# Compressed interaction network on one core: two of the three layers' sums over d move from VectorE to ScalarE

## The reference

```python
x0 = embeddings                       # (B=2048, M=32, D=16), gathered from 32 tables
xk = x0
for W in (W0, W1, W2):                # (32, 32, 64), (32, 64, 64), (32, 64, 64)
    xk = relu(einsum('bmd,bhd,mhk->bkd', x0, xk, W))
    outs.append(sum(xk, axis=2))      # sum over d
z = concatenate(outs, axis=1)         # (2048, 192)
h = relu(concatenate([z, dense_ctx], axis=1) @ W_top1 + b_top1)   # 512
h = relu(h @ W_top2 + b_top2)                                     # 256
y = h @ W_top3
```

## Time and profile before

| | |
|---|---|
| median of 3 runs | 1193.18 us (1192.31 to 1193.81) |
| profiled execution | 1192.97 us, its span 1191.2 us |
| granted TensorE clock, mean over the span | 0.991 |
| busy, share of the span | PE 94%, DVE 94%, ACT 62%, POOL 77% |

### The profile page before, as it was taken

The page is one execution under the profiler, slowest core; times in us unless marked ns, Lnnn a source line. Parts: engine busy times, 40 slices in busy tenths (PEclk is TensorE's granted clock), DMA queues, the critical chain, the costliest instruction groups (busy, mean ns, idle before and its releaser), DMA issues.

```text
span 1191.2 us, 14658 instructions
## 1 busy us (share of the span) xinstructions
PE 1121.3 (94%) x5312; PEld 393.6 (33%) x5312; DVE 1118.8 (94%) x521; ACT 733.9 (62%) x1361; POOL 918.8 (77%) x640
## 2 busy tenths in 40 slices
PE   0488899999999999999999999999999999999997
PEld 0122223333333333333333333333333333333333
DVE  0487999999999999999999999999999999999995
ACT  0343666676667667665766766576676657657653
POOL 6688888888888888888888888888888888885400
PEclk9888999999999999999999999999999999999999
DMA  5887787667678766677876666788666778876300
GB/s 110 190 176 146 158 171 155 138 132 144 140 157 171 157 141 141 132 144 150 172 163 136 143 134 145 144 171 168 139 140 134 143 145 169 166 144 144 61 1 1
DMA packets 76216, 167.25 MB, mean 140 GB/s; under 512 B 21776, under 2 KB 39072, under 8 KB 76144
## 3 DMA queue, kind: packets, MB, share of 16 engines
q1 hardware_dynamic: 59216, 161.95, 64.8%
q0 software_dynamic: 16384, 4.23, 3.6%
q10 hardware_dynamic: 544, 0.14, 0.1%
HBM read 157.86 MB, written 8.40 MB: 140 GB/s over the span
## 4 chain that ended last, share of the span: by engine, by line
PE 86%; POOL 3%; DVE 3%; DMA 3%; issue 3%; ACT 1%; SPq 1%; DVEq 0%
PE acc L600 80%; POOL x_rows L254 3%; DVE p_dve L516 3%; PE acc L672 3%; PE acc L658 1%; PE acc L660 1%; DMA q_tile<-x_of_steps 1%; ACT xb L317 1%; DMA x_rows<-in_table,ids_s 1%; PE acc L680 1%; DMA spread<-x_of_steps 1%; SPq L192 1%; DMA x_of_steps<-x_rows 0%; SPq L219 0%; DVE z L543 0%
## 5 line engine op out<-in xcount | busy, mean ns | idle before, releaser
L600 PE MATMUL acc<-p_dve,w_s 128*64 128x512 f32 x3840 | 863.2, 598 | 22.5 <-DVE p_dve L516 21.8
L254 POOL DMA_INDIRECT x_rows<-in_table,ids_s x512 | 493.7, 964 | 146.1 <-issue 131.2
L516 DVE TENSOR_TENSOR p_dve<-spread,xb 128x3072 f32<-128x3072 f32 (+2 forms) x224 | 572.2, 2682 | 2.9 <-issue 2.9
L516 DVE TENSOR_TENSOR p_dve<-spread,xa 128x2048 f32<-128x2048 f32 (+1 forms) x192 | 501.5, 2730 | 16.6 <-issue 9.1
L600 PEld LDWEIGHTS acc<-p_dve,w_s 128*64 128x64 f32 x3840 | 267.9, 137 | 571.5 <-issue 467.2
L317 ACT ACTIVATE xb<-acc 32x512 f32<-32x512 f32 x512 | 288.8, 564 | 71.6 <-DVE p_dve L516 65.5
L266 POOL TENSOR_TENSOR p_l<-spread,q_tile 128x2048 f32<-128x2048 f32 x60 | 272.7, 4573 | 11.0 <-DMA q_tile<-x_of_steps 10.4
L308 ACT ACTIVATE xa<-acc 64x512 f32<-64x512 f32 x256 | 145.9, 570 | 189.6 <-PE acc L600 155.0
L277 POOL TENSOR_TENSOR p_pool<-spread,x_s 128x1024 f32<-128x1024 f32 x64 | 152.2, 2378 | 94.7 <-PE acc L600 45.9
L600 PE MATMUL acc<-p_l,w_s 128*64 128x512 f32 (+1 forms) x640 | 152.5, 612 | 41.6 <-DVE p_l L556 41.6
L326 ACT ACTIVATE x_s<-acc 64x512 f32<-64x512 f32 x256 | 151.5, 592 | 8.3 <-ACT y_row L449 4.8
(11 more groups left out here) (18 smaller groups left out, 151.1 us busy)
## 6 DMA issues: line engine op xcount, KB each, us to landing
spread<-x_of_steps SPq DMA_DIRECT2D x248, 512.0 KB, 17.4
q_tile<-x_of_steps SPq DMA_DIRECT2D x128, 128.0 KB, 11.4
x_rows<-in_table,ids_s POOLq DMA_INDIRECT x512
x_of_steps<-x_rows SPq DMA_DIRECT2D x64, 128.0 KB
spread<-x_of_steps SPq DMA_DIRECT2D x16, 256.0 KB, 5.4
w_s<-in_w SPq DMA_DIRECT2D x2, 512.0 KB, 5.7
wt<-in_w_top SPq DMA_DIRECT2D x1, 512.0 KB, 6.5
z_all<-in_dense_t ACTq DMA_DIRECT2D x16, 8.0 KB, 8.2
```

What stands on the lines that cost most here:

```text
L254: nc.gpsimd.indirect_dma_start(out=x_rows[:, s % 2, i * DIM:(i + 1) * DIM], out_offset=None, in_=table, in_offset=bass.IndirectOffsetOnAxi ...
L516: nc.vector.tensor_tensor(p_dve[:, to:to + n, :], spread[:, s % 3, tile:tile + n, :], over(x[:], n), ALU.mult).then_inc(dve_made, n)
L600: last = nc.tensor.matmul(acc[b * K:(b + 1) * K, :], w, prod[:, b * BLK:(b + 1) * BLK], start=start, stop=stop)
```

## The change

Layers 0 and 1 (the first and the second) get their sums on ScalarE. Instead of one eviction of 512 columns, 32 evictions of 16 columns each are issued, every one with an accumulator output that gives the sum of its 16 results to one column of `z`. In the built program each such eviction is two ScalarE instructions, the ACTIVATE and one that writes the accumulator's value to `z`; the listing of the order below has one row for both. VectorE keeps only the sums of the third layer (`sums_2`). `sums(s, 0)` stands behind `x1_b(s)` where `out_0(s)` stood ahead of it, `x2_a(s-1)` stands ahead of `out_2(s-2)`, the accumulators are given back by `z_made` in place of `out_ready`, and the MLP's first two stages move from behind chunk 5 to behind chunk 8 of L1.

```diff
-MLP1_AFTER, MLP2_AFTER, MLP3_AFTER = 5, 5, 13
+MLP1_AFTER, MLP2_AFTER, MLP3_AFTER = 8, 8, 13
...
-            def out_0(s):
+            def sums(s, layer, acc):
                 if s > 0:
-                    act.wait_ge(z_made[0], s)
-                nc.scalar.activation(out_l[:, 0, :], acc0[:], ACT.Relu).then_inc(out_ready[0], 1)
+                    act.wait_ge(z_made[layer], s)
+                if s % 2 == 0 and s >= 4:
+                    act.wait_ge(z_moved, s // 2 - 1)
+                for i in range(SB // 2):
+                    cols = slice(i * DIM, (i + 1) * DIM)
+                    last = nc.scalar.activation(out_l[:, layer, cols], acc[:, cols], ACT.Relu,
+                                                accum_out=z[:, s // 2 % 2, layer, s % 2, i:i + 1])
+                last.then_inc(z_made[layer], 1)
...
                 x1_b(s)
+                sums(s, 0, acc0)
+                if s >= 1:
+                    x2_a(s - 1)
                 if s >= 2:
                     out_2(s - 2)
-                if s >= 1:
-                    x2_a(s - 1)
...
                     x2_s(s - 1)
-                    out_1(s - 1)
+                    sums(s - 1, 1, acc1[(s - 1) % 2])
...
                     x1_a(s + 1)
                     x1_s(s + 1)
-                    out_0(s + 1)
...
                 for c, n in GROUPS_L1:
-                    if c == NT:
-                        sums(s, 0)
-                        if s >= 2:
-                            sums(s - 2, 1)
...
                     if c == 0 and s > 0:
                         pe.wait_ge(x1b_ready, s)
-                        pe.wait_ge(out_ready[0], s)
+                        pe.wait_ge(z_made[0], s)
```

More of the change, by code:

```diff
@@ L153, in build_kernel @@
         x2b_ready = sem("x2b_ready")
-        out_ready = [sem(f"out{n}_ready") for n in range(3)]
+        out2_ready = sem("out2_ready")
         z_made = [sem(f"z{n}_made") for n in range(3)]
@@ L388, in x2_s @@
                 relu_s(acc1[s % 2], 2, x2s_ready)
[L390 to L394, removed]
             def out_2(s):
@@ L400, in out_2 @@
                     act.wait_ge(z_made[2], s)
-                nc.scalar.activation(out_l[:, 2, :], acc2[:], ACT.Relu).then_inc(out_ready[2], 1)
+                nc.scalar.activation(out_l[:, 2, :], acc2[:], ACT.Relu).then_inc(out2_ready, 1)
             def move_sums(t, to, k, n):
@@ L457, in _ @@
             x1_s(0)
-            out_0(0)
             for s in range(STEPS):
@@ L492, in _ @@
             x2_s(STEPS - 1)
-            out_1(STEPS - 1)
+            sums(STEPS - 1, 1, acc1[(STEPS - 1) % 2])
             mlp3(TILES - 2)
@@ L536, in layer2, with sums_2 @@
                 products(s, 2, c, n)
-            def sums(s, n):
+            def sums_2(s):
                 if s % 2 == 0 and s >= 4:
                     dve.wait_ge(z_moved, s // 2 - 1)
[L542 to L545, removed]
+                dve.wait_ge(out2_ready, s + 1)
+                nc.vector.reduce_sum(z[:, s // 2 % 2, 2, s % 2, :],
+                                     out_l[:, 2, :].rearrange("p (i d) -> p i d", d=DIM),
+                                     AX_X).then_inc(z_made[2], 1)
             def first_layer_products(s):
@@ L581, in _ @@
                 if s >= 2:
-                    sums(s - 2, 2)
+                    sums_2(s - 2)
                 if s >= 1:
@@ L587, in _ @@
                 if c == NT:
[L588 to L591, removed]
+                    sums_2(STEPS - 2)
                 layer2(STEPS - 1, c, n)
-            sums(STEPS - 1, 2)
+            sums_2(STEPS - 1)
         @block.tensor
@@ L622, in layer1 @@
                 if c == 0 and s >= 2:
-                    pe.wait_ge(out_ready[1], s - 1)
+                    pe.wait_ge(z_made[1], s - 1)
                 if c != POOL_CHUNK:
@@ L636, in layer2 @@
                 if c == 0 and s > 0:
-                    pe.wait_ge(out_ready[2], s)
+                    pe.wait_ge(out2_ready, s)
                 if c != POOL_CHUNK:
@@ L652, in mlp1 @@
                 pe.wait_ge(x1b_ready, min(2 * t + 5, STEPS))
-                pe.wait_ge(out_ready[0], min(2 * t + 5, STEPS))
+                pe.wait_ge(z_made[0], min(2 * t + 5, STEPS))
                 if t > 0:
@@ L667, in mlp2 @@
                 pe.wait_ge(x1b_ready, min(2 * t + 6, STEPS))
-                pe.wait_ge(out_ready[0], min(2 * t + 6, STEPS))
+                pe.wait_ge(z_made[0], min(2 * t + 6, STEPS))
                 for n in range(H2 // P):
```

## The result

The kernel after takes 1396.32 us (median of 4 runs, 1392.38 to 1397.86), the kernel before 1192.74 (1191.93 to 1193.81): a ratio of 1.170, 95% interval 1.168 to 1.173. The profiled execution took 1395.96 us.

The account below looks back on a forecast made before the run. VectorE was taken as the bound at 34.6 us a turn, PE next at 34.1; ScalarE would become the bound: 1193.0 + 30 x 4.3 - 2 = 1320 us. Range for 8 in 10: 1200 to 1415; likeliest case 1240 to 1400.

Parts of the forecast that it names:

- p = 0.26 us: Time from one 16-column ScalarE eviction to the next: ACTIVATE 0.160 to 0.18 us plus 0.10 for the accumulator write; ends 0.16, 0.34.
- in a run without a pointer operand nothing overlaps: ScalarE evictions without a pointer operand follow at their full duration, 0.60 us for 512 columns.
- rival (a): Evictions on ScalarE are cheap, p under 0.192 us; PE is the bound, 1176 up to 1190 us; chance 0.13.
- the rows of 512 columns: ScalarE evictions to `x_s` came every 0.60 us, against 520 ns by the skill page; held against its overlap.
- 22.3 + 64 p = 38.9 us: ScalarE's turn: 22.3 us left without `out_0` and `out_1`, plus 64 evictions at 0.26 us, against 34.6.
- No wait lengthens ScalarE's chain: In a 38.9 us turn TensorE's work is ready before ScalarE wants it, with 4 to 5 us to spare.
- its bound (3.5 us a turn): PE's loss at 1.2 GHz for 7 us behind its wait; `layer0` at 35 instead of 32, nothing added.
- they hide there: In turns 0 and 1 the 8.3 us of sums fit in ScalarE's waits for PE, 14.5 and 9.4 us.
- rival (c): ScalarE's p lies between, 0.19 to 0.22 us: 1191 to 1238 us, second instruction 0.03 to 0.05; chance 0.07.
- The ceiling of 1176 us: Best case: VectorE's turn falls to 33.4 us, PE takes over at 34.1; gain 15 us plus about 2 in the tail.
- my count of chunks and stages: PE's work in a turn: 37 chunks, 31.8 us, plus 2.3 us of MLP stages, 34.1 us.
- the disappearance of `xa <- PE`: Sign expected in the profile after: ACT's waits for PE ahead of `xa` gone.

## Why the prediction was right in sign and off in size

**The price of an eviction, p = 0.26 us: one number for two.** Undisturbed, p is 0.157 us, below the lower end of 0.16 and well below the 0.192 at which ScalarE keeps up; the step "in a run without a pointer operand nothing overlaps" failed: plain evictions of 16 columns come every 0.064 us, where the shortest is shown with 0.18, and the second instruction adds 0.09. Beside gathers p is about 0.36 (11.6 / 32). The mean over a turn, (11.6 + 5.4) / 64 = 0.27, is close to the forecast's value by luck. So the price stood where rival (a) wants it, below 0.192, by other parts than it named; the holes took it away again. Rival (a) had beside it the Trainium skill, "ScalarE: Activation LUTs", "What ACT_TABLE_LOAD costs", by which 16 columns come every 106 ns as an estimate; on the overlap the page was nearer than the rows of 512 columns that I held against it, and the measured 64 ns is lower still.

**ScalarE's stream, 22.3 + 64 p = 38.9 us.** It came out at 40.3 (after) and 40.2 (MLP stages behind chunk 12). The evictions are nearly right in the mean (17.0 us instead of 16.6); 0.85 us a turn is more "issue" ahead of the copies and `y_row` behind them (16.1 + 6.4 us in 26.5 turns in the view of waits). That goes with the gathers too: neither the kernel before nor the one without gathers has such a wait there.

**"No wait lengthens ScalarE's chain" failed.** The prediction had `layer0` done near 32 us after the end of `x1_a` and wanted at 36.6. In the turn shown it is done at 37.8 (743.95 - 706.13). The sums of layer 0 end at 19.0 instead of 15.4, 3.6 us later, because nearly all holes fall on this set; the MLP's stage takes 1.8 us more from there on, since it runs at 1.2 GHz behind a wait of 5 us. That is more than the slack of 4 to 5. The clock was named and its bound (3.5 us a turn) was wide enough; what was missing was that it would meet a path without slack. By the view of waits the path adds 1.2 us a turn to the stream, 34 us of the 203.

**The sum.** Forecast 30 x 4.3 - 2 = 127. Measured: 28 turns x (40.3 - 34.6) = 160 for the stream, 28 x 1.2 = 34 for the path, 8.6 in the start-up, 2 at the end. So the mis-sized terms are the turn of ScalarE (+5.7 instead of +4.3), the wait put at nothing, and the start-up: "they hide there" failed, since the two sets of sums there, beside gathers too, took 13.3 and 15.6 us instead of 8.3. (By the same sum rival (c) ends at some 1244 us, not at 1238; nothing rests on it.)

**The ceiling of 1176 us failed as well.** TensorE's turn is 34.4 to 34.6 us (the kernels without accumulators and without gathers), not 34.1; where in the turn the 0.3 to 0.5 us lie that my count of chunks and stages missed, I did not measure. VectorE's turn was 34.61, so there was little to win by relieving it: 7.6 us in one run without accumulators, which leaves the sums out. The kernel without gathers, with cheap sums, stands at the time of before: its turns give back 5 us, and its start-up, where the gathers are still there, takes 5.6 us more (L1(2) at 125.68 instead of 120.06). The page of the kernel before had a sign of this that the prediction did not use, the chain that ended last:

```profile
PE 86%; POOL 3%; DVE 3%; DMA 3%; issue 3%; ACT 1%; SPq 1%; DVEq 0%
```

VectorE's saving itself was right: 33.6 us busy, 33.4 forecast.

**What the profile was to show.** VectorE's and TensorE's waits for ScalarE came as said, 4.4 and 4.7 us a turn. ACT's near 100% did not, nor the disappearance of `xa <- PE`.

**What stays open.** That gathers make the holes, and that the number of instructions from their start on decides, is shown. That this number is a stock of instructions which runs dry is the reading that fits; no view shows the stock. By what means a gather on GpSimd slows ScalarE is not shown either. The profile counts 61 fetches of 8 KB on the instruction queue q14 (30 before, for 4032 fewer instructions), two a turn, against nine holes a turn, so a hole is not one such fetch. The transfers of the gathered rows are not it either, as far as one turn tells. The DMA queues of the kernel after, from 724.2 to 725.2 us (packets, MB, share):

```profile
q0 software_dynamic: 84, 0.02, 12.5%
```

That is the gathers' queue, busier than in the 5.8 us ahead (172 packets), while the last evictions of `sums(s, 0)` start at full pace (724.22 to 724.92); from 712 to 718.4 us it has no packet at all, and by then one hole is over and the next has begun. What goes with the holes is GpSimd's work on the gathers, 712.77 to 722.52, with a lag of 1.7 us at the end and 3.7 at the start. No run separated the two.

## What to carry to other kernels

Price a run of short instructions by the distance of starts in a like run, not by the duration of a longer one, and count how many follow one another: beside another engine's indirect DMAs 33 cost nothing or a few tenths of a us here, and 64 took twice as long. Before moving work off the busiest engine, check the next one to the tenth of a us (34.6 against 34.4 to 34.6 here); where they are equal there is little to win and every new wait is a loss. And follow the moved work's end, not only its length: TensorE waited for the last of the 64 instructions.

## What was not expected of the hardware

- 32 plain evictions of 16 columns from PSUM to SBUF start 0.064 us apart, though each is shown with 0.18 us or more; with an accumulator 0.157 us apart.
- From the start of GpSimd's indirect DMAs on ScalarE ran 27 to 40 instructions at full pace (25 to 46 in the other kernels) and then a few at a time between holes of 0.4 to 0.9 us; 64 instructions took 11 to 12 us instead of 5.4. The holes ended with the gathers, in most turns 1.7 us behind the last.
- Behind a wait of 5 us in every turn TensorE's granted clock was 0.52 for the 3.6 us of the MLP's first stage, and 1.00 again behind it.
